# FP4 feed-forward of a transformer layer on one core: the last chunks of the transposed h get the unused PSUM bank, the third piece of gate and up takes the first piece's banks, and the last tile's h is quantised in two parts

## What is computed

```
def fp4_quant_dequant(x):
    xb = x.reshape(shape[:-1] + (shape[-1] // BLOCK, BLOCK))          # BLOCK = 16
    scale = jnp.max(jnp.abs(xb), axis=-1, keepdims=True) / 6.0
    scale = jnp.maximum(scale, jnp.float32(1e-12))
    xn = xb / scale
    idx = jnp.searchsorted(_MID, jnp.abs(xn))
    q = _GRID[idx] * jnp.sign(xn) * scale
...
gate = fp4_linear(x, w_gate)        # fp4_linear quantises both of its operands
y = fp4_linear(x, w_up)             # w_gate, w_up: 1408 x 512
h = jax.nn.silu(gate) * y
return fp4_linear(h, w_down)        # w_down: 512 x 1408
```

## Time and profile before

| | |
|---|---|
| median of 3 runs | 3919.64 us (3914.42 to 3921.28) |
| profiled execution | 3916.59 us |
| its span, first to last instruction | 3914.8 us |
| TensorE matmuls busy over the span | 3762.7 us (96%) |
| TensorE weight loads busy | 2697.4 us (69%) |
| VectorE / ScalarE / GpSimd busy | 2629.6 (67%) / 1213.3 (31%) / 933.1 us (24%) |
| mean granted TensorE clock | 0.985 |
| first FFN matmul | at 2313.7 us |

### The profile page before, as it was taken

One profiled execution on the slowest core, in us unless ns is written; L12 is line 12 of the kernel. 1 busy time (PEld: TensorE's weight loads), 2 busy tenths in 40 slices (PEclk: granted clock), 3 DMA queues, 4 the chain that ended last, 5 costly groups with the idle time before them and its releaser, 6 DMA issues. The chain is left out here.

```text
span 3914.8 us, 63781 instructions
## 1 busy us (share of the span) xinstructions
PE 3762.7 (96%) x21836; PEld 2697.4 (69%) x21836; DVE 2629.6 (67%) x3826; ACT 1213.3 (31%) x2312; POOL 933.1 (24%) x462
## 2 busy tenths in 40 slices
PE   7999999999999999999999989999999999999998
PEld 5556556557556556556565558888888888888887
DVE  5666665665666665665665657777777777777776
ACT  2451441442532532532523522222222222222221
POOL 0461550550641641632632620000000000000000
PEclk9999999999999999999999999999999999999999
DMA  5425425426335335235336440111111111111110
GB/s 172 119 62 181 98 77 182 94 78 184 79 102 157 79 118 157 66 113 158 75 124 185 135 143 27 32 32 32 32 32 32 32 32 32 32 32 32 32 32 27
DMA packets 178222, 337.02 MB, mean 86 GB/s; under 512 B 42432, under 2 KB 50112, under 8 KB 176832
## 3 DMA queue, kind: packets, MB, share of 16 engines
q1 hardware_dynamic: 153504, 275.75, 24.9%
q10 hardware_dynamic: 24480, 58.21, 4.4%
HBM read 213.92 MB, written 118.43 MB: 85 GB/s over the span
## 5 line engine op out<-in xcount | busy, mean ns | idle before, releaser
L1452 PE MATMUL f_ps<-wgu,xqt 128*128 128x512 f32 (+1 forms) x4608 | 991.8, 373 | 16.1 <-DVE h L1334 14.7
L1452 PEld LDWEIGHTS f_ps<-wgu,xqt 128*128 128x128 f32 x4608 | 840.3, 188 | 152.1 <-DVE h L1334 30.0
L883 ACT ACTIVATE pt<-ps_st 128x512 f32<-128x512 f32 (+3 forms) x1152 | 551.5, 527 | 658.7 <-PE ps_st L1014 509.1
L605 DVE TENSOR_REDUCE mx<-ps_s 128x1 f32<-128x640 f32 (+3 forms) x576 | 553.6, 961 | 202.2 <-PE ps_s L985 199.2
L543 POOL TENSOR_TENSOR stage<-stage,pt 128x1536 f32<-128x1536 f32 (+2 forms) x176 | 518.8, 2948 | 15.5 <-POOL stage L543 0.5
L1463 PE MATMUL f_ps_o<-wd,hqt 128*128 128x512 f32 x2112 | 512.1, 395 | 2.2 <-DVE hqt L1341 2.2
L541 POOL TENSOR_TENSOR stage<-pt 128x1792 f32<-128x1792 f32 x64 | 258.5, 4040 | 1013.9 <-ACT pt L883 1013.9
L1463 PEld LDWEIGHTS f_ps_o<-wd,hqt 128*128 128x128 f32 x2112 | 392.0, 188 | 81.2 <-DVE hqt L1341 2.6
L956 PE MATMUL ps_dense<-arena,wa 128*128 128x512 f32 x1536 | 389.9, 400 | 12.8 <-DVE rob L653 6.3
L605 DVE TENSOR_REDUCE mx<-ps_dense 128x1 f32<-128x512 f32 x448 | 219.1, 489 | 218.6 <-PE ps_dense L985 213.6
L956 PEld LDWEIGHTS ps_dense<-arena,wa 128*128 128x128 f32 x1536 | 280.0, 190 | 73.5 <-issue 10.4
(11 more groups left out here) (125 smaller groups left out, 4853.2 us busy)
## 6 DMA issues: line engine op xcount, KB each, us to landing
qk_scratch<-stage SPq DMA_DIRECT2D x128, 512.0 KB, 2.9
stack<-qk_scratch SPq DMA_DIRECT2D x192, 256.0 KB
arena<-qk_scratch SPq DMA_DIRECT2D x192, 256.0 KB
xs<-in_L_attn_x SPq DMA_DIRECT2D x64, 256.0 KB, 3.8
rob<-in_L_attn_x ACTq DMA_DIRECT2D x64, 256.0 KB, 2.8
acc_scratch<-rob ACTq DMA_DIRECT2D x64, 256.0 KB, 2.1
xt<-in_L_attn_x SPq DMA_DIRECT2D x64, 256.0 KB, 2.6
at<-acc_scratch SPq DMA_DIRECT2D x64, 256.0 KB, 2.6
```

The lines of the kernel that those rows point to most:

```text
L605: nc.vector.tensor_reduce(mx[:, h * ST + q:h * ST + q + 1], scores_bank(p, n)[:, 0:(q + 1) * P], axis=AX.X, op=ALU.max, negate=True).then_ ...
L883: nc.scalar.activation(exps(kt)[:, h, q - kt * P:q - kt * P + n], ps_st[:, w % ST_RING, 0:n], ACT.Exp, scale=SCALE).then_inc(st_exp, 1)
L1452: last = nc.tensor.matmul(ps[:, [0, 1, 1][c], gu, 0:n].rearrange("p (j n) -> p j n", n=P), xqt[:, a, k], wgu[:, b, gu * FC + f // P:gu * F ...
```

## The change

Four edits. (1) A new PSUM tensor `ps_h` in the unused bank takes the last three chunks of the transposed h. (2) Piece 2 of gate and up goes to slot 0, no longer to slot 1 (`SLOT`); its wait now is for the product of piece 0, and gate_up(t, 0) of the next tile waits for the product of piece 2. (3) The bank of `ps_h` is one that the attention's output projection used, so the wait for that (`shared.projected`) moves up, ahead of tile 1's transposes. (4) For tile 63 alone, VectorE quantises columns 0 to 1023 and then 1024 to 1407, each as the whole chain of eight operations; the product of piece 2 stands inside the first chain, the addition of tile 62 inside the second; ScalarE's `abs_h` is split likewise, and the last `down` starts with chunks 0 to 7 and waits ahead of chunk 8 for the rest.

```
+    ps_h = ctx.enter_context(nc.psum_tensor("f_ps_h", [P, 512], F32))
+    SLOT = [0, 1, 0]
+    def ht_bank(n):
+        return ps[:, 2].rearrange("p a b -> p (a b)") if n == 0 else ps_h[:, :]
...
+        def quantise_last_h(n, aside):
+            f, k = TR[n]
+            cols, of_scales = slice(f * P, (f + k) * P), slice(f * P // BLK, (f + k) * P // BLK)
+            quantise(h_chain, (NT - 1 + n) * LINKS, h[:, cols], ht[:, cols], hd[:, cols], ha[:, cols], hs[:, :, of_scales],
+                     h_t, h_abs, NT + n, (h_d, NT + n, h_q), aside=aside)
...
         step(NT - 1, last=True)
-        quantise_h(NT - 1)
-        add(NT - 2)
+        dve.wait_ge(h_mul, NT * 3 - 1)
+        quantise_last_h(0, lambda: times_up(NT - 1, 2))
+        dve.wait_ge(h_mul, NT * 3)
+        quantise_last_h(1, lambda: add(NT - 2))
         low_of_h(NT - 1, 0)
...
             pe.wait_ge(xt_lo, t + 1)
-            if not first:
-                pe.wait_ge(ht_lo, t * 2 - 2)
             if first:
                 pe.wait_ge(shared.wgu_in, len(PIECES) * DMA)
+            else:
+                pe.wait_ge(h_mul, t * 3)
             gate_up(t, 0)
-            if not first:
-                pe.wait_ge(h_mul, t * 3)
             gate_up(t, 1)
+            if second:
+                shared.projected(pe)
             if not first:
                 pe.wait_ge(h_q, t)
                 transpose_h(t - 1, 0)
-                pe.wait_ge(h_mul, t * 3 + 1)
                 transpose_h(t - 1, 1)
-            pe.wait_ge(h_mul, t * 3 + 2)
+            pe.wait_ge(h_mul, t * 3 + 1)
             gate_up(t, 2)
...
-        pe.wait_ge(h_q, NT)
-        transpose_h(NT - 1, 0)
-        pe.wait_ge(h_mul, NT * 3)
-        transpose_h(NT - 1, 1)
-        pe.wait_ge(ht_lo, NT * 2)
+        for n in range(2):
+            pe.wait_ge(h_q, NT + n)
+            transpose_h(NT - 1, n)
+        pe.wait_ge(ht_lo, NT * 2 - 1)
         pe.wait_ge(o_add, NT - 1)
-        down(NT - 1)
+        down(NT - 1, last_tile=True)
```

More of the change, by code:

```diff
@@ L1333, in times_up @@
             dve.wait_ge(s_done, t * 3 + c + 1)
-            nc.vector.tensor_tensor(h[:, f:f + n], silu[:, c, 0:n], ps[:, [0, 1, 1][c], 1, 0:n],
+            nc.vector.tensor_tensor(h[:, f:f + n], silu[:, c, 0:n], ps[:, SLOT[c], 1, 0:n],
                                     ALU.mult).then_inc(h_mul, 1)
@@ L1339, in low_of_h @@
             dve.wait_ge(ht_hi, t * 2 + n + 1)
-            slot = ps[:, [2, 0][n]].rearrange("p a b -> p (a b)")[:, 0:k * P].rearrange("p (k n) -> p k n", k=k)
+            slot = ht_bank(n)[:, 0:k * P].rearrange("p (k n) -> p k n", k=k)
             nc.vector.tensor_tensor(hqt[:, 1, f:f + k], slot, hqt[:, 0, f:f + k].bitcast(F32),
@@ L1362, in step @@
                 quantise_x(dve, t + 1)
-            times_up(t, 2)
-            if not last:
+                times_up(t, 2)
                 low_of_x(dve, t + 1)
@@ L1400, in silu_of @@
             act.wait_ge(gu_full, t * 3 + c + 1)
-            nc.scalar.activation(silu[:, c, 0:n], ps[:, [0, 1, 1][c], 0, 0:n], ACT.Silu).then_inc(s_done, 1)
+            nc.scalar.activation(silu[:, c, 0:n], ps[:, SLOT[c], 0, 0:n], ACT.Silu).then_inc(s_done, 1)
         def high_of_h(t, n):
@@ L1426, in scalar @@
         step(NT - 1, last=True)
-        abs_h(NT - 1)
+        for n, (f, k) in enumerate(TR):
+            act.wait_ge(h_t, NT + n)
+            cols = slice(f * P, (f + k) * P)
+            nc.scalar.activation(ha[:, cols], ht[:, cols], ACT.Abs, scale=ROUND).then_inc(h_abs, 1)
         high_of_h(NT - 1, 0)
@@ L1442, in transpose_h @@
             for i in range(k):
-                last = nc.tensor.transpose(ps[:, [2, 0][n], i // 4, i % 4 * P:(i % 4 + 1) * P],
-                                           ht[:, (f + i) * P:(f + i + 1) * P], ident[:, :])
+                last = nc.tensor.transpose(ht_bank(n)[:, i * P:(i + 1) * P], ht[:, (f + i) * P:(f + i + 1) * P], ident[:, :])
             last.then_inc(ht_full, 1)
@@ L1451, in gate_up @@
                 for i, (k, a, b) in enumerate(terms):
-                    last = nc.tensor.matmul(ps[:, [0, 1, 1][c], gu, 0:n].rearrange("p (j n) -> p j n", n=P), xqt[:, a, k],
+                    last = nc.tensor.matmul(ps[:, SLOT[c], gu, 0:n].rearrange("p (j n) -> p j n", n=P), xqt[:, a, k],
                                             wgu[:, b, gu * FC + f // P:gu * FC + (f + n) // P, k * P:(k + 1) * P],
@@ L1455, in gate_up, with down @@
             last.then_inc(gu_full, 1)
-        def down(t, next_x=False):
+        def down(t, next_x=False, last_tile=False):
             terms = [(k, a, b) for k in range(FC) for a, b in ((0, 0), (0, 1), (1, 0))]
             for i, (k, a, b) in enumerate(terms):
+                if last_tile and (k, a, b) == (TR[1][0], 0, 0):
+                    pe.wait_ge(ht_lo, NT * 2)
                 if next_x and i == X_AT:
@@ L1488, in step @@
                     pe.wait_ge(shared.wd_in, DOWN_LOADS * DMA)
-                    shared.projected(pe)
                 else:
```

## The result

The changed kernel takes 3885.05 us (median of 6 runs, 3878.68 to 3887.03), the kernel before 3918.4 us (6 runs, 3914.42 to 3921.28). The ratio is 0.9912, with a 95% interval of 0.99 to 0.9925. The forecast was 3884.7 us, in a range of 3877 to 3893.

The account below looks back on a forecast made before the run. TensorE was taken to bound the FFN, with VectorE having slack. 29.8 (loop) - 1.2 (tile 0) + 4.6 (end) + 1.7 (clock) = 34.9 us, off the 3919.64 us median: 3884.7 us, range 3877 to 3893.

Parts of the forecast that it names:

- The bound and the wait: FFN loop: TensorE is the bound, its one wait per tile being piece 2 for VectorE's product of piece 1.
- 0.48 us a tile: Piece 2 in slot 0 removes that wait, worth the loads' 0.48 us over tiles 1 to 62: 29.8 us.
- The cheaper prices: Rivals on the loop's wait: only 0.21 us a tile, 3901.5 us (0.05), or 0.37 with refill, 3891.6 us (0.05).
- The meetings with VectorE: Inside each tile, other TensorE waits on VectorE stay met; slack before x's transposes falls from 1.27 to 0.79 us.
- the slower rival: Loop: VectorE's PSUM reads stretch, costing time beyond 1.27 us; 3984 us if they double; chance 0.02.
- Tile 0: Removed wait joins the later wait for x, 2.9 us idle; likely clock fall costs 1.2 us (bounds 0 and 1.7).
- The end: Splitting the last h lets the last down's load start 4.6 us sooner (bounds 3.5 and 5.2).
- The straight line over widths: End: VectorE chain time at 6.5 ns a column gives 8.40 us for 1024 columns, 4.24 for 384.
- The clock in the last down: With idle time broken up, the clock rather stays up, gaining 1.7 us (bounds 0 and 2); a fall nearly as likely.
- The sum: Whole kernel: 29.8 - 1.2 + 4.6 + 1.7 = 34.9 us gained.
- nothing moves in the loop: Rival: VectorE's round is the true bound, the wait shifts to x's transposes, only the end gains: 3914.6 us; chance 0.03.
- the two clock terms: Clock's effect: minus 1.2 us for a fall at tile 0, plus 1.7 us for staying up in the last down.

Follow-up runs that it names:

- the repetition: The changed kernel itself run once more, unaltered, beside other variants on one chip: 3884.02 us, ratio 0.9914 to the kernel before.
- fillers: Changed kernel plus unread matmuls in TensorE's idle times, in tile 0 and at the end: 3882.84 us; only the end's nine, with x quantised sooner: 3880.48 us.
- one more operation: Changed kernel plus one unused 512-wide VectorE operation per tile from tile 1 on, before quantising x: 3884.72 us in a single run.
- two and three more operations: Changed kernel plus two or three unused VectorE operations per tile from tile 1 on, before quantising x: 3898.06 and 3939.76 us in single runs.
- x sooner: Changed kernel with tile 1's x quantised ahead of the product of piece 1 in tile 0: 3879.12 us, ratio 0.9894 to the kernel before.
- end only: Kernel before the change plus only the split of the last h, slots and banks as before: 3913.29 us, ratio 0.9985.
- wait back: Changed kernel, but piece 2 again waits for the product of piece 1, new slot and bank kept: 3913.28 us, ratio 0.9988 to the kernel before.
- no new bank: Changed kernel without the new bank: last three chunks of transposed h go to slot 1, piece 2 to slot 0; 3928.87 us, ratio 1.0028 to before.

## Why the prediction was right, point by point

- **The bound and the wait.** Right, and shown: with the wait alone put back, a tile is as long as before.
- **0.48 us a tile.** Right: 24.754 - 24.273 = 0.481. Over tiles 1 to 62 the forecast was 29.8; the trace shows 29.29 for tiles 2 to 62 and another 0.48 in tile 1 beneath the clock's fall. The cheaper prices (0.21, and 0.37, the estimate with a refill by the Trainium skill, "TensorE: Matmul & The Clock Gate", sections "Single matmul latency" and "Back-to-back issue gap") both fall; the trace doesn't bear out that estimate. Behind transposes the load has hardly any lead (piece 2's first matmul is let go at 3801.48, its load at 3801.45), and the loads' delay was the price.
- **The meetings with VectorE.** Right: no new wait, 0.79 us from the quantised x to the load of its transposes. What I called slack was a little short of it: the experiments show 0.9. I had left out that a load behind a wide matmul runs ahead, by 0.23 us here, of which some 0.1 came back. So the slower rival would begin to cost at about 0.9 us, but nothing in the kernel reaches it.
- **Tile 0.** Right that the wait only moves (3.10 us by the loads, 2.79 by the matmuls, 2.9 said) and that the clock would fall. The size was off: it cost 0.48 in tile 0 and 1.64 in tile 1, 2.1 instead of 1.2 and over the upper bound of 1.7. I had taken a part of the price of one fall; here it slowed the four transposes too and lasted into tile 1. In the repetition tile 0 was as long as before and tile 1 lost 1.6, so the price is one of the single execution.
- **The end.** 4.6 said, 4.8 measured. The straight line over widths gave 8.40 + 4.24 = 12.64 us for the two chains; from 3852.64 to 3865.17 they took 12.53, with the product of piece 2 and the addition of tile 62 inside their waits, as said.
- **The clock in the last down.** Wrong: I expected it to stay up, worth 1.7 us, and in this trace and in its repetition it fell (9.41 us, as before). Nine traces have this end without fillers, but not with the same idle time. In six TensorE waits 2.40 us ahead of the last three transposes: there the clock fell in three (the changed kernel, its repetition and the one with one more operation) and stayed up in three (two and three more operations, x sooner). In the other three (end only, wait back, no new bank) the wait of piece 2, or of the transposes ahead of it, is still there, TensorE reaches the end later and idles only 1.6 to 1.9 us, and the clock stayed up in all. So the 0.48 us that piece 2 gains in tile 63 come back as idle time. "Nearly as likely" was the right thing to say, but the sum took the full 1.7.
- **The sum.** 34.9 said; 29.8 - 2.1 + 4.8 - 0 = 32.5 against 32.4 in the trace. The medians moved by 33.4. That the forecast's 3884.7 lies so near to 3885.05 is luck: the two clock terms were off by 2.6 together, and the kernel before had a median of 3918.4 in the longer series instead of the 3919.64 from which I subtracted.

The rivals "nothing moves in the loop" and "slower" are out by the empty list of waits. Nor did VectorE's reads of PSUM stretch: both low parts of h take 1.69 us in the loop and the addition 0.68, before and after. What no run here settles is why the mean tile is 24.273 us in some traces and 24.280 in others of the same code; all 61 tiles of a trace show the one or the other, and it is 0.4 us over the loop.

## What to carry to other kernels

When a product waits only because its bank is still being read, look at what the engine does a few steps later in the same order: here one unused bank and another slot turned a wait in each of 62 tiles into none, while the other slot without the bank made the kernel slower. Price a wait by what is in the pipeline ahead of it: behind short transposes the delay of the weight load counted in full (0.48 of 0.48), behind wide matmuls 0.2 us of it was free (0.27 of 0.49, 0.89 of 1.09). And when you take a wait away ahead of another one, count what the longer idle time does to the clock: here 2.1 us in one trace and 1.6 in its repetition, which an earlier start of the other engine's work gave back with interest (46.84 us up to tile 2 became 42.47).

## What the runs showed of the hardware

**The clock fell near idle times shorter than 3 us, and not in every execution.** In tile 0, with 2.79 us of wait ahead of four transposes and 1.41 us behind them, the granted clock fell to 0.50 in all of seven traces. With the shorter waits of before (1.13 and 1.41 us by the matmuls) it fell in one of three, and with 0.53 us or less ahead (the fillers, x sooner) in none of three. At the end, with 2.40 us ahead of three transposes and 0.59 us behind, it fell in three of six, by the same instructions; with 1.6 to 1.9 us ahead, in none of three. Where it fell at all, it fell sooner or later and lasted longer or shorter: the price was from 1.4 us (tile 1 with two more operations, 25.87 against 24.18 + 0.27) to 2.9 us (with three, 27.96 against 24.18 + 0.89). So a comparison of single executions should count it apart. Three traces are few, and what decides between a fall and none at 2.40 us is not shown.

**How far a weight load runs ahead depends on what is before it.** Behind a 512-wide matmul the load of the next transpose was issued 0.23 us ahead of it (3786.26 and 3786.49), behind a transpose that of the next wide matmul 0.03 us (3801.45 and 3801.48). A late load cost its whole delay in the second place and 0.2 us less than that in the first.
